# Mixture of experts on one core: third and fourth token tile turned by VectorE, first and second by TensorE

## The reference

```
x = x + tanh(g_xattn) * attn(layernorm(x), ctx)          # per batch: sigmoid(Q'K/16) as scores
h = layernorm(x)
t = rmsnorm(h) * norm_w;  logits = t @ gate_w.T + gate_b
top 4 of 16 experts per token, softmax over the four -> G
expert e:  u = t @ w1[e].T + b1[e];  a = min(u[even], 7);  b = clip(u[odd], -7, 7)
           y = (a * sigmoid(1.702 a) * (b + 1)) @ w2[e].T + b2[e]
x = x + tanh(g_ffn) * (h + sum over e of G[:, e] * y_e)
```

## Time and profile before

| | us |
|---|---|
| median of 3 timed runs (lowest to highest) | 847.19 (846.18 to 848.17) |
| the profiled execution | 851.6 |
| its span | 849.8 |
| TensorE busy | 780.2 |
| VectorE busy | 504.1 |
| ScalarE busy | 445.9 |
| GpSimd busy | 311.3 |

### The profile page before, as it was taken

One profiled execution on the slowest core, in us unless ns is written; L12 is line 12 of the kernel. 1 busy time (PEld: TensorE's weight loads), 2 busy tenths in 40 slices (PEclk: granted clock), 3 DMA queues, 4 the chain that ended last, 5 costly groups with the idle time before them and its releaser, 6 DMA issues.

```text
span 849.8 us, 16473 instructions
## 1 busy us (share of the span) xinstructions
PE 780.2 (92%) x3972; PEld 651.1 (77%) x3973; DVE 504.1 (59%) x1006; ACT 445.9 (52%) x771; POOL 311.3 (37%) x290
## 2 busy tenths in 40 slices
PE   5999998248999999999999999999999999999984
PEld 2544554237888899988889888899998988898873
DVE  2677666415676665566576664756557575746540
ACT  3445533115566575556557655646556565646540
POOL 0157575730433325233324323334333333325212
PEclk9999999559999999999999999999999999999997
DMA  8565654051586576348558654556535554544212
GB/s 288 177 198 176 230 163 111 20 139 51 125 229 145 125 214 165 58 138 208 123 163 212 173 114 131 148 136 148 148 57 151 107 150 131 156 123 74 37 25 38
DMA packets 107766, 116.98 MB, mean 138 GB/s; under 512 B 11808, under 2 KB 77344, under 8 KB 107744
## 3 DMA queue, kind: packets, MB, share of 16 engines
q1 hardware_dynamic: 88896, 77.32, 29.3%
q0 software_dynamic: 18848, 39.40, 23.6%
HBM read 88.06 MB, written 28.94 MB: 138 GB/s over the span
## 4 chain that ended last, share of the span: by engine, by line
PE 80%; DVE 7%; issue 7%; ACT 3%; DMA 1%; POOL 0%; DVEq 0%; ACTq 0%; POOLq 0%; SPq 0%; another core or an unknown queue 0%
PE ps L525 37%; PE ps L474 25%; PE ps L378 7%; PE ps L389 6%; PE ps L453 3%; DVE W1l L1028 1%; DVE uu L1017 1%; PE ps L406 1%; DVE hv L1019 1%; DVE bv L1015 1%; ACT hTh L698 1%; ACT bw L678 1%; PE ps L397 1%; ACT sg L675 1%; DVE ps L988 1%
## 5 line engine op out<-in xcount | busy, mean ns | idle before, releaser
L525 PE MATMUL ps<-xTh,W1h 128*128 x768 | 260.7, 339 | 10.2 <-issue 6.9
L525 PE MATMUL ps<-xTh,W1l 128*128 x768 | 255.0, 332 | 0.0
L525 PE MATMUL ps<-xTl,W1h 128*128 x768 | 255.0, 332 | 0.0
L1175 POOL DMA_INDIRECT out<-ys,dgI x75 | 118.8, 1584 | 309.2 <-ACT ys L657 285.2
L525 PEld LDWEIGHTS ps<-xTh,W1h 128*128 128x128 f32 x768 | 145.9, 190 | 20.4 <-issue 15.3
L525 PEld LDWEIGHTS ps<-xTh,W1l 128*128 128x128 f32 x768 | 145.8, 190 | 5.4
L525 PEld LDWEIGHTS ps<-xTl,W1h 128*128 128x128 f32 x768 | 146.0, 190 | 5.1
L474 PE MATMUL ps<-W2h,hTh 128*128 x300 | 120.3, 401 | 5.6 <-DVE hTl L1023 5.6
L474 PE MATMUL ps<-W2l,hTh 128*128 x300 | 118.1, 394 | 0.0
L474 PE MATMUL ps<-W2h,hTl 128*128 x300 | 117.9, 393 | 0.0
L657 ACT ACTIVATE ys<-ps,dgI 128x512 f32<-128x512 f32 x75 | 51.7, 689 | 124.2 <-DVE ps L988 120.2
(11 more groups left out here) (130 smaller groups left out, 995.4 us busy)
## 6 DMA issues: line engine op xcount, KB each, us to landing
W1f<-in_wts SPq DMA_DIRECT2D x64, 512.0 KB
W2f<-in_wts SPq DMA_DIRECT2D x32, 512.0 KB
X<-in_x SPq DMA_DIRECT2D x8, 512.0 KB, 6.3
Kt<-in_ctx SPq DMA_DIRECT2D x8, 512.0 KB
Vt<-in_ctxT SPq DMA_DIRECT2D x8, 512.0 KB
rows<-tt SPq DMA_DIRECT2D x8, 512.0 KB
out<-base SPq DMA_DIRECT2D x8, 512.0 KB
b2s<-in_bias SPq DMA_DIRECT2D x16, 256.0 KB
```

What stands on the lines that cost most here:

```text
L525: m = e.matmul(P_[i % 2][:, 0:64 * w], (W1h, W1l)[wl][:, i, 2 * k + h, :], (xTh, xTl)[xl][:, bass.ds(par, 1), k, 0:64 * w], start=(t == 0) ...
L1175: e.indirect_dma_start(out, bass.IndirectOffsetOnAxis(dgI[:, j, 0:1].bitcast(I32), axis=0), ys[j][:], None, compute_op=ALU.add).then_inc(d ...
```

## The change

1. The features of a row in `rows` are stored in the order 4m + c in place of 128c + m (c the block of 128 features, m the place in it). `centred` writes with this stride, and the router's weights `gwT` are loaded in the same order, by four copies.
2. Tiles 0 and 1 are gathered by whole rows as before. TensorE turns them, but takes each of its four blocks as every fourth element of `xg[j]`. Both turns stand at the first part: tile 0 ahead of the second layer, tile 1 behind it.
3. Tiles 2 and 3 are gathered as four pieces of 128 features each, one indirect transfer per piece, so that partition 32q + s of piece i holds quarter q of the row of token 32i + s. VectorE turns such a tile with one instruction that transposes blocks of 32x32, into the same bank `PX`. The row numbers for this come from `row4`, which GpSimd computes once from `idx4`, and `idx4` is filled by 16 copies that SyncE issues after `idx` has landed, ahead of the last base store.
4. The tiles of the first unit are gathered into `ys`, and turned by TensorE from there, so `xg` is free for the second unit at once.
5. ScalarE copies the gates of the previous unit itself (`keep_gates`) and waits itself for the scatters that have to have landed (`added_back`).

```diff
@@ SyncE, ahead of the loop
             e.dma_start(idx[:, 0:TE, :], places[:, 0, :, :]).then_inc(d_idx0, 16)
...
+            e.wait_ge(d_idx0, 16)
+            e.wait_ge(d_idx, 16)
+            for i in range(4):
+                for q in range(4):
+                    e.dma_start(idx4[32 * q:32 * q + 32, i, 0:(E + 1) * TE, :], idx[32 * i:32 * i + 32, 0:(E + 1) * TE, :]).then_inc(d_idx4, 16)
             store_base(B - 1)
@@ TensorE
+            def turn_in(j, r):
                 e.wait_ge(e_xl, r)
                 for c in range(4):
-                    m = e.transpose(P_[:, 128 * c:128 * c + 128], xg[j][:, 128 * c:128 * c + 128], idm)
+                    m = e.transpose(PX[:, 128 * c:128 * c + 128], xg[j][:].rearrange("p (m c) -> p c m", c=4)[:, c, :], idm)
                 m.then_inc(e_tx, 1)
...
                     if i == 0:
                         turned_in(0)
                         second_layer(e.snap(u * 4 + 4))
-                    if i < 3:
-                        turned_in(i + 1)
+                        turned_in(1)
...
+                e.reg_add(turned, turned, now[F_NT])
+                with e.If(e.snap(now[F_NT], min_val=0, max_val=4) < 2):
+                    e.reg_add(turned, turned, 1)
@@ ScalarE
-                    e.wait_ge(e_dg, e.snap(u + 1))
-                    e.sem_inc(e_ga, 1)
+                    added_back()
...
                 e.copy(bcur[:], b1s[:, bass.ds(x_, 1), :, :].rearrange("p o h c -> p (o h) c")).then_inc(e_bc, 1)
-                e.wait_ge(e_bc, e.snap(u + 1))
+                keep_gates()
+                e.wait_ge(e_bc, e.snap(u * 2 + 2))
@@ VectorE
-                e.scalar_tensor_tensor(tt[b % 2][:, j, :], x1[b % 2][:, j, :], mv1[:, b, j, 0:1], nwb[:], ALU.subtract, ALU.mult).then_inc(v_u, 1)
+                e.scalar_tensor_tensor(tt[b % 2][:, j, :].rearrange("p (m c) -> p c m", c=4), x1[b % 2][:, j, :].rearrange("p (c m) -> p c m", c=4),
+                                       mv1[:, b, j, 0:1], nwb[:].rearrange("p (c m) -> p c m", c=4), ALU.subtract, ALU.mult).then_inc(v_u, 1)
...
+                def turn(i):
+                    with e.If(more > LESS[i]):
+                        e.reg_add(landed[i], landed[i], 64)
+                        e.wait_ge(d_g[i], e.snap(landed[i], min_val=64, max_val=64 * NTILES))
+                        e.wait_ge(e_xl, e.snap(e.snap(split, min_val=4, max_val=NTILES + 24) + 1))
+                        e.transpose(PX[:].rearrange("p (i c t) -> p i c t", i=4, c=4), xg[i][:].rearrange("p (i s c) -> p i c s", i=4, c=4)).then_inc(e_tx, 1)
...
                 turned_in(1)
+                turn(2)
...
                         if i < 3:
                             turned_in(i + 1)
+                        if i == 1:
+                            turn(3)
@@ GpSimd
+            e.wait_ge(d_idx4, 256)
+            e.tensor_scalar(row4[:, :, 0:(E + 1) * TE], idx4[:, :, 0:(E + 1) * TE, 0].bitcast(I32), 4.0, C[:, C_PIECE:C_PIECE + 1], op0=ALU.mult, op1=ALU.add).then_inc(e_src, 1)
...
             def gather(j):
-                e.indirect_dma_start(xg[j][:], None, rows, bass.IndirectOffsetOnAxis(srcI[:, j, 0:1].bitcast(I32), axis=0)).then_inc(d_g[j], 16)
+                for i in range(4):
+                    e.indirect_dma_start(xg[j][:, 128 * i:128 * i + 128], None, rows.rearrange("r (q h) -> (r q) h", q=4),
+                                         bass.IndirectOffsetOnAxis(src4[:, j - 2, i:i + 1], axis=0)).then_inc(d_g[j], 16)
...
-                place(row(fut), e.snap(u + 3))
-                gathers(fut)
+                place2(row(fut), e.snap(u * 2 + 5))
+                gathers2(fut)
+                place4(e.snap(row(fut) + 2), e.snap(u * 2 + 6))
+                gathers4(fut)
```

More of the change, by code:

```diff
@@ L648, in act, with keep_gates, added_back @@
             e.reg_mov(done, 0)
[L649 to L650 removed]
+            for r in was:
+                e.reg_mov(r, 0)
             load_fields(e, now, 0, 0)
             load_fields(e, nxt, 1, 0)
+            def keep_gates():
+                row = e.snap(was[F_ROW], min_val=0, max_val=(E + 1) * TE - 1)
+                e.copy(gcur[:], idx[:, bass.ds(row, 4), 1:2]).then_inc(e_bc, 1)
+            def added_back():
+                with e.If(e.snap(done, min_val=0, max_val=NTILES) > 0):
+                    e.wait_ge(d_s, e.snap(e.snap(done, min_val=1, max_val=NTILES) * 16))
+                    e.sem_inc(e_ga, 1)
             def gated(j):
@@ L1145, in count, with gathers2, gathers4 @@
                 return e.snap(regs[0], min_val=0, max_val=4)
-            def gathers(regs):
+            def gathers2(regs):
+                with e.If(count(regs) > 0):
+                    e.reg_add(given, given, 2)
+                    for j in range(2):
+                        gather2(j)
+            def gathers4(regs):
                 more = count(regs)
-                for j in range(4):
-                    with e.If(more > LESS[j]):
+                for j in range(2, 4):
+                    with e.If(more > j):
                         e.reg_add(given, given, 1)
                         gather(j)
-            e.wait_ge(e_tx, 4)
-            place(row(nxt), 2)
-            gathers(nxt)
+            place2(row(nxt), 3)
+            gathers2(nxt)
+            place4(e.snap(row(nxt) + 2), 4)
+            gathers4(nxt)
             e.wait_ge(d_zero, 16)
```

110 lines of the change are left out of this document (75 added, 35 removed).

## The result

| | before | after |
|---|---|---|
| median of the timed runs | 847.19 us (843.03 to 848.17, 7 runs) | 853.07 us (851.27 to 854.54, 7 runs) |
| profiled execution, its span | 851.6, 849.8 | 852.03, 850.2 |
| TensorE, VectorE, ScalarE, GpSimd busy | | 768.1, 534.7, 447.2, 404.5 us |
| table load issued to first first-layer matmul | 14.28 us | 25.34 us |
| loop: first first-layer matmul to the start of the last second layer | 641.53 us | 638.15 us |

The ratio is 1.0076 (95% interval 1.006 to 1.0091): the kernel is 0.8% slower, and 855.0 had been forecast. (The ratios here are those on record for each set of runs; they differ a little from the quotient of the two medians, which is 1.0069 here.) The last three rows are the whole account: +11.06, -3.38 and -3.3 us make +4.4, where the medians say +5.9.

What follows compares the result with a forecast made beforehand. The prediction took TensorE to bound the kernel, busy 636.56 of 655 us in the loop. It summed 851.6 - 13.0 + 0 + 7.7 + 0.5 + 12.6 = 859.4 us, less 4.4 for timed runs: 855.0, range 839 to 865.

Steps and rivals of the forecast that it cites:

- the likeliest case: TensorE's turns: strided weight loads cost a price like VectorE's, giving 855 us (849 to 864), chance 0.45.
- the prediction's own signs: Profile after: wrong if weight loads stay at 0.14 us or TensorE's idle time in the loop grows by over 5 us.
- Term 1: Expert loop: 25 turns leave TensorE, 13.0 us gained, low bound 10.
- Term 2: Expert loop: VectorE gets 25 turns of 1.0 us, hidden in its waits for ScalarE, cost 0.
- The rival "VectorE is what TensorE waits for": Loop units of three and four tiles: VectorE's turns hold up TensorE, 12 us on top, 867 or 855, chance 0.09.
- Term 3: Ahead of the loop: 16 copies in SyncE's queue delay the base store and ScalarE behind it, cost 7.7 us.
- Term 4: Attention half: the centring write becomes strided, cost 0.5 us (0 to 0.7).
- Term 5: TensorE's turns of the first two tiles: strided weight loads take longer, 0.25 us for each of 50 turns, cost 12.6 us.
- The first rival, free loads: TensorE's turns: strided weight loads cost nothing, 842.4 us (838 to 846), faster, chance 0.34.

Runs made afterwards that it cites:

- store_first_plain_count: Changed kernel, base store ahead of the 16 copies, GpSimd's second-unit row gathers ahead of its wait for them, turned-tile count without branch or divisions: 838.88 us, ratio 0.9918.
- store_first: Changed kernel with the last base store issued ahead of the wait and the 16 copies: 845.84 us, ratio 0.9995.
- copies_in_before: Kernel before with only the wait and the 16 copies, unused, put ahead of the last base store: 858.94 us, ratio 1.0134.
- strided_before: Kernel before with all 75 TensorE turns reading every fourth float of a row: ratio 0.9997.
- late_sequencer: Changed kernel with 12 register moves added at the end of TensorE's loop body, none of which the trace holds: ratio 1.0103.

## Why the prediction was right

The number was right, 855.0 against 853.07, and so was the sign; the likeliest case that it was attached to was not. Two terms were off (3 and 5), two costs and one gain were missing, and they cancelled: the hit is luck. By the prediction's own signs it was wrong: TensorE's idle time in the loop grew by 6.3 us, where over 5 was to mean so, and there is a new wait of TensorE for VectorE. Four loads of a turn take 0.61 to 0.67 us in most turns, where 0.56 or 0.8 to 0.9 had been named.

- **Term 1, 25 turns off TensorE, -13.0: about right as far as a remainder can tell, its side cost was not.** The branch cost 5.4 us in the kernel before, and taking it out of the changed one saved 4.2 (the loops of store_first_plain_count and after, without their first units). What is left of the loop's -3.38 when this, the VectorE jam (+2.9) and the strides (+1 at most) are taken out is -10.5 to -12.7. That is a remainder and no measurement: it holds whatever else changed in the loop. Unit 6, a wide one, gained 0.92 us by its two turns. The step that failed reads "less the three register instructions added at the loop's end (up to 1 us in all)". There was a branch among them, and behind it TensorE ran dry in the units whose last part is short or whose load of the fields is long.
- **Term 2, VectorE's 25 turns at no cost: wrong by 2.9 us.** The turn took 1.12 us where 1.0 was estimated, and there is cover for it in 22 units. The cover of the earlier trace rows was read in a unit that doesn't convert weights. At the end of an expert conversions of 1.2 us fill it, and where four tiles follow there, both turns come on top. The step that failed reads "the excess of 0.1 to 0.2 us delays only work that the next TensorE part doesn't ask for (a part needs the gate of two parts earlier)": a unit's first part also asks for the low halves of all its tiles, and that of the fourth came late. The rival "VectorE is what TensorE waits for" was true of two units, and half of its price was the clock.
- **Term 3, the stretch ahead of the loop, +7.7: right in the order of SyncE's queue, 11.1 in size.** The store was forecast to leave at 181.5 and left at 181.45, by two errors that cancelled: the copies took 0.63 us each, as the 128-partition copy of the earlier trace rows does, and not 0.40 (10.1 in place of 6.4), but the profiled attention half ended 4 us earlier. It was to land at 187.8, 6.3 us later, and ScalarE did start at 187.78; but the store had landed 3.1 us after its issue, and the other 3.2 us were ScalarE's register loads, which the term doesn't hold. Against its own table load the loop started 11.06 us later.
- **Term 4, the centring, +0.5: not seen.** The write did get slower, about 1.15 us where it was 0.75, but the table load is issued at 167.86 us in store_first and at 167.84 in copies_in_before, of the same set of runs. In the later sets the kernels without the change even have it later (172.20 to 174.08) than those with it (167.46 to 170.95), which no term explains.
- **Term 5, the strided loads, +12.6: this is the step that failed.** It held that "the loads stand back to back, so anything that they take longer shows". Each did take 65 ns longer, close to the 80 that VectorE's rows had suggested. It didn't show: strided_before's interval ends at 1.0011, 0.9 us for 75 turns, where 19 had been due. The first rival, free loads, was the true one. The Trainium skill's rule ("SBUF — State Buffer", section "Door 1: The DMA port swizzle") gives both answers, a penalty for each new 16-byte line and a free stride of four fp32. The load's 205 against 140 ns agree with the first half, and the kernel's time with the second.
- **What no term held:** the end. From the start of the last second layer the changed kernels take 19.5 to 21.0 us (nine profiles) and those without the change 21.9 to 23.4 (five). Of the 3.3 us between the two main profiles 1.1 lie on TensorE, up to the issue of the last scatter, and go with the clock. Before, and after, in the stretch from the last second layer's start:
```profile
826.00:830.00 4.00, 3.17 (x8) 2.50 (x9) 0.56 (x1) 0.00 (x0) 0.00 (x0) 0.50 0.00 0
830.00:835.00 5.00, 5.00 (x18) 4.02 (x17) 0.70 (x1) 0.69 (x1) 0.22 (x1) 0.73 0.01 3
```
```profile
829.00:834.00 5.00, 3.52 (x10) 2.81 (x11) 0.66 (x2) 0.70 (x2) 0.00 (x0) 0.74 0.00 0
834.00:839.00 5.00, 5.00 (x21) 4.07 (x21) 1.40 (x2) 0.98 (x2) 1.47 (x1) 0.92 0.02 3
```
  The other 2.2 lie behind the issue of the last scatter: 7.0 to 7.4 us to the end in the nine, 9.3 to 9.7 in the five. GpSimd's wait for that transfer is over 4.7 and 4.8 us after its issue in the two. Then comes GpSimd's last record but for semaphores, a drain of 4.41 us before and 2.08 after, and the 2.3 us between them are the difference. Why it is shorter stays open.

By this account the rival of free loads should have come out at 842.4: it did not, since the branch, the jam and the longer copies took 4.2 to 5.4, 2.9 and 3.4 us of it, and the end gave 3.3 back: 849.6 to 850.8, against 853.07 measured. Some 2 to 3 us are not accounted for.

What stays open: what the pauses of ScalarE are, and how much of late_sequencer's 1.0103 against 1.0076 is theirs; why the load of a unit's fields takes twice as long in every second unit, and what moving it would bring. That ScalarE's gate has room in the narrow units was not tried by delaying it; that the sequencer's records show no wait there is the evidence for it.

## What to carry to other kernels

Before moving work off the busiest engine, look at what the move adds to that engine's own loop end: where the last piece of work in the loop is short, a branch there costs time, and a removed instruction gives none. The sequencer's records tell whether it waits there or works. The name behind the arrow in a row of waits is inferred: see when that instruction ended before you build on it. A cover seen in one iteration is no cover in the iteration that has the extra work, so look for the fullest one. A wait put into a queue costs all that stands behind it: put the store that others wait for ahead of the copies that nobody needs yet.

## What the runs showed of the hardware

- An `If` around one register operation at the end of TensorE's loop, in the kernel before: 0.3 to 0.5 us in eleven of 23 units, 0.2 at most in the others. Its compare-and-branch takes the sequencer 0.21 us (median of 24, changed kernel). Two integer divisions in its place are not much cheaper (0.07 to 0.20 us less in the narrow units, where dropping both frees 0.3 to 0.4).
- The load of five fields from SBUF into registers of TensorE's sequencer: 0.60 to 0.62 us in the even units, 1.24 to 1.29 in the odd ones (changed kernel).
- TensorE's weight load of 128 x 128 fp32 with the elements 16 bytes apart: 205 ns, dense 140; the matmuls of the turn 281 against 272 ns.
- VectorE's 32 x 32 transposes of 128 x 512 fp32, a strided read in SBUF to PSUM: 1.12 us; a pass over the same number of elements 0.69.
- A wait of 2.9 us between matmuls was followed by a stretch at the lower clock in six profiles (some 3 us long in the changed kernel's) and by none in two, for the same instructions.
- Pauses of ScalarE with nothing to wait for, 7.3 to 13.8 us in all, in the four profiles of changed kernels on one chip; none in those on two others.
- A copy of 32 partitions x 2312 bytes costs SyncE's queue 0.63 us, no less than one of 128 partitions.
